# Two-layer attention and expert kernel on one Trainium2 core: the weighted sums of V of a step, in two halves of their columns behind the two pairs of scores

## The chip, the cores and the metric

The kernel runs on one core of one Trainium2 chip, as one program. The time is the device time of an execution in microseconds (us), taken on that core; three runs of the kernel before gave 772.68, 773.29 and 773.67 us, and the median of them, 773.29 us, is the time before. A profile of one execution stands beside them. Engines go by the short names of the profile: PE is TensorE's matmuls, PEld its weight loads, DVE is VectorE, ACT is ScalarE, POOL is GpSimd, SP is the engine that issues most of the DMAs.

## The reference

The input is one sequence of 1024 tokens with 256 features. Two layers run one after the other, each an attention block and a block of experts, with a layer norm ahead of and behind each block and a residual sum:

```
x = x + LN(attention0(LN(x)))      # 16 heads of 16, causal, with biases
x = x + LN(experts0(LN(x)))        # 32 experts, 4 per token, plus a shared one
x = x + LN(attention1(LN(x)))      # 16 heads of 16, causal, rotary positions
x = x + LN(experts1(LN(x)))        # RMS norm, 32 experts, 4 per token, shared one
```

The part that the change touches is the same in both attention blocks, for each head:

```
scores = q @ k.T / 4               # 1024 x 1024, only keys up to the query count
probs  = softmax(scores)
y      = probs @ v
```

## The kernel before, in words

Attention is cut into groups of four heads (`HG`) and chunks of 512 queries (`CH`). A phase is one group with one chunk, so there are four groups by two chunks = 8 phases (`PHASES`, numbered 0 to 7), and a step (`STEPS`) is one phase with one block of 128 keys. A phase of the first chunk has 4 steps, all on the diagonal, with 512, 384, 256 and 128 query columns; one of the second chunk has 8 steps, 4 of 512 columns and 4 on the diagonal, which stand by turns. That makes 48 steps in a layer.

For each step the scores stand transposed, keys by queries, in four banks of PSUM, one per head, made by `scores(st, p)` (L936 to L947) in two pairs of heads, p = 0 and 1. The first pair of a step waits until the exponentials of the first pair of the step before have emptied its two banks, the second pair likewise. ACT (`exps`, L1295 to L1302) turns each pair into probabilities with one instruction and writes them to one of three buffers `probs` (`PB`). On the diagonal POOL clears the upper triangle (L735). `weigh(st)` (L949 to L961) multiplies the probabilities by V: for each of the four heads the weights are V's block of 128 keys by 32 columns (16 of V, a column of ones, zeros), the moving operand is the probabilities of that head, and the result goes to 32 partitions of one bank (`RB`) that collects the sums of a whole phase. So the four heads of a step stand side by side in the array, 32 columns each. A matmul on 32-bit data is two instructions in the profile, so a `weigh` is 8 instructions of L959. After the last step of a phase ACT copies that bank to SBUF (`pv_copy`, L1304 to L1308), and the first `weigh` of the next phase waits for that copy.

Meanwhile the row maxima that the softmax needs are worked out a few phases ahead: a "max" unit (L865 to L881) is a product of queries and keys into one of three rotating banks, plus a small product that adds the causal mask (L880), and DVE reduces the bank to its maxima (L1563). Three banks means that PE can be at most three units ahead of DVE. Other units (`rows`, `turn`, `yT`, `proj`, `fT`, `logits`) go through the same three banks.

All this runs in an order written out once, by `schedule()` (L154 to L190). PE, ACT and DVE each walk through the same list and pick out their own part, and each engine works strictly in that order. For every step the list has: the scores of pair 0, one unit, the scores of pair 1, one unit, the `weigh` of the step two before (`HEAD_START` = 2), and then the remaining units of that step (3 to 5 in all while there are maxima left, `RATE`). ACT's copy at the end of a phase stands where the `weigh` of its last step stands in the list. In layer 0 the maxima run out at the end of phase 4; after that a step has at most one or two units.

```
        for p in range(2):
            if st < NSTEP:
                out.append(("score", st, p))
            out += more[:1]
            more = more[1:]
        if st >= HEAD_START:
            out.append(("weigh", st - HEAD_START))
        out += more
```

Of the kernel before, what the change touches and what calls it, by code (L numbers as in the profile page):

```python
# [21 lines left out]
HG = 4  # L22
NG = H // HG
CH = 512
# [129 lines left out]
def schedule():  # L154

    def maxima(g, c):
        return [("max", g, u) for u in range(CHUNK_UNITS[0] * c, CHUNK_UNITS[c])]

    own = maxima(0, 1) + [("rows", 0, 1)]
    out = maxima(0, 0) + [("rows", 0, 0)] + own[:OWN_AHEAD]
    own = own[OWN_AHEAD:]
    later = [x for g, c in PHASES[NC:] for x in maxima(g, c)]
    for st in range(NSTEP + HEAD_START):
        n, s = (STEPS[st][0], st - PHASE_AT[STEPS[st][0]]) if st < NSTEP else (NPH, st - NSTEP)
        more = []  # L170
        if n == 0 and s < TPC - 1:
            more, own = own[:FIRST_RATE], own[FIRST_RATE:]
        elif n == 0:
            more = own + later[:FIRST_MORE]
            later = later[FIRST_MORE:]
        elif n in RATE:
            more, later = later[:RATE[n]], later[RATE[n]:]
        more += [("rows", g, c) for (g, c), at in ROWS_AT.items() if at == (n, s)]
        if s == TURN_STEP and n >= 1:
            more.append(("turn", n - 1, 0))  # L180
        more += FRONT_AT.get((n, s), ())
        for p in range(2):
            if st < NSTEP:
                out.append(("score", st, p))
            out += more[:1]
            more = more[1:]
        if st >= HEAD_START:
            out.append(("weigh", st - HEAD_START))
        out += more
    return out  # L190

# [89 lines left out]
def build(nc, a, out):  # L281
    ctx = ExitStack()
    with ctx:
# [518 lines left out]
        def _(pe):  # L802
# [17 lines left out]
            for L in range(2):  # L820
# [125 lines left out]
                                       QA[0:KX, h, c * CH + off:(c + 1) * CH], start=True, stop=True)  # L946
                    mm.then_inc(S(f"sc{L}"), 1)  # L947

                def weigh(st):  # L949

                    n, g, c, b = STEPS[st]
                    off = max(0, b * P - c * CH)
                    pe.wait_ge(S(f"exp{L}"), 2 * st + 2)
                    if DIAGONAL[st]:
                        pe.wait_ge(S(f"masked{L}"), masked_steps(st))
                    if b == 0 and n >= 1:
                        pe.wait_ge(S(f"pv_sb{L}"), n)
                    for x in range(HG):
                        mm = pe.matmul(ps[32 * x:32 * x + 32, RB, off:CH], V[:, b, HG * g + x, :],  # L959
                                       probs[:, st % PB, x, off:CH], start=(b == 0), stop=(b == TPC * (c + 1) - 1))  # L960
                    mm.then_inc(S(f"pv{L}"), 1)  # L961

                for x in SCHEDULE:
                    if x[0] == "max" and x[2] == 0:
                        pe.wait_ge(S(f"qa_rows{L}_{x[1]}"), 16 * 2 * NPROD)
                    if x == ("score", 0, 0):
                        pe.wait_ge(S(f"v_sb{L}"), NT)
                        pe.wait_ge(S("v_pad"), 1 + 2 * L)
                        pe.wait_ge(S(f"qk_sb{L}"), 2 * KD * NC)
                        pe.wait_ge(S("k_ones"), 16 * NSH * (L + 1))  # L970
                    if x[0] == "score":
                        scores(*x[1:])
                    elif x[0] == "weigh":
                        weigh(x[1])
                    else:
                        unit(x)
                    if L == 0 and x[:2] == ("max", 0) and x[2] in LATE_K:
                        qk_product(*LATE_K[x[2]])
# [217 lines left out]
        def _(act):  # L1196
            for L in range(2):
# [112 lines left out]
                for x in SCHEDULE:  # L1310
                    if x[0] == "score":
                        exps(*x[1:])
                        if L == 1 and x[1:] == (0, 1):
                            split(1, 1, 0)
                        if x[1:] in ((1, 1), (2, 1)):
                            split(1, x[1] - 1, 1)
                    elif x[0] == "rows":
                        _, g, c = x
                        act.wait_ge(S(f"unit{L}"), UNIT_NO[x] + 1)
                        if g >= 1:  # L1320

                            act.wait_ge(S(f"max_rows{L}_{c}"), 16 * NSH * g)
                        nc.scalar.activation(mT[:, c * CH:(c + 1) * CH], ps[0:NSH * HG, UNIT_NO[x] % RB, :],
                                             ACT.Copy).then_inc(S(f"maxT{L}"), 1)
                        if g == 0:
                            act.wait_ge(S(f"maxT{L}"), c + 1)
                            max_rows(act, L, 0, c)
                        if (g, c) == (0, 0):
                            if L == 0:
                                qk_out(7)  # L1330
                                split(1, 1, 0)
                            else:
                                split(1, 0, 0)
                    elif x[0] == "weigh":
                        if x[1] + 1 in PHASE_AT:
                            pv_copy(STEPS[x[1]][0])
                srest, erest = SHARED[L] - SFULL[L] * P, HALF
                nsc = SFULL[L] + 1
# [748 lines left out]
```

## Time and profile before

| what | value |
|---|---|
| three runs, median | 773.29 us (772.68 to 773.67) |
| the profiled execution, span from first to last instruction | 771.2 us |
| median of the runs minus that span | 2.1 us |
| PE busy, share of the span | 674.1 us, 87% |
| PEld busy | 437.5 us, 57% |
| DVE busy | 485.2 us, 63% |
| ACT busy | 323.1 us, 42% |
| mean granted clock of TensorE | 0.954 |

No time of the profiled execution other than its span is shown; what lies around the span (start and end of the program) is taken as the 2.1 us by which the median of the runs is longer. The span falls into attention of layer 0 (to about 190 us), its experts (to about 415 us), attention of layer 1 (to about 600 us) and its experts. Busy matmuls are pipelined: a matmul's duration in the profile includes the time until its last result has come out, so two neighbours overlap, and the distance from one start to the next says how long the engine is really held.

### The profile page before, as it was taken

Reading aid. Unit: us, or ns where it says so; the run is one execution under the profiler, and the core shown is the slowest. Engines: PE = TensorE matmul, PEld = TensorE weight load, DVE = VectorE, ACT = ScalarE, POOL = GpSimd, SP = SyncE. Lnnn points to the kernel's source line nnn. Section 1 sums busy time; section 2 is a strip of 40 time slices with the busy share of each in tenths; the row PEclk is TensorE's granted clock in tenths of the full one; section 3 lists DMA queues with packets and bytes.
Section 4 is the critical chain, followed back from the end, with each engine's and each line's share of the span. In section 5 each row is a group of like instructions: output and inputs, shape, how many; then the busy total and the mean of one; then the engine's idle time right before and its main releaser. Section 6 shows DMA issues by size and latency. Waiting matters only on the chain.

```text
span 771.2 us, 13393 instructions
## 1 busy us (share of the span) xinstructions
PE 674.1 (87%) x4388; PEld 437.5 (57%) x4388; DVE 485.2 (63%) x1354; ACT 323.1 (42%) x684; POOL 249.5 (32%) x294
## 2 busy tenths in 40 slices
PE   3988999999569999999983978999998899999991
PEld 2533443344437899999962533343343455999980
DVE  4389899544683344444476788899527886243457
ACT  3553464765124233222241533565676231333322
POOL 3041011210137677444430083011211002767630
PEclk9999999999778999999995979999999999999995
DMA  3433210060008999999780245003000540399762
GB/s 99 135 124 126 77 34 2 5 216 28 27 1 262 303 328 327 294 311 315 261 267 0 75 144 165 15 2 115 2 2 1 164 133 14 116 291 308 244 204 91
DMA packets 60294, 108.60 MB, mean 141 GB/s; under 512 B 11194, under 2 KB 37131, under 8 KB 60100
## 3 DMA queue, kind: packets, MB, share of 16 engines
q1 hardware_dynamic: 52532, 93.86, 37.4%
q0 software_dynamic: 7632, 13.86, 5.5%
q8 instruction: 37, 0.61, 0.3%
q14 instruction: 29, 0.24, 0.1%
q10 hardware_dynamic: 64, 0.03, 0.0%
HBM read 79.98 MB, written 19.79 MB: 129 GB/s over the span
## 4 chain that ended last, share of the span: by engine, by line
PE 61%; DVE 26%; ACT 4%; DMA 4%; issue 3%; SPq 1%; ACTq 0%; DVEq 0%; POOLq 0%
PE ps L1132 17%; DVE mx L1563 11%; PE ps L959 7%; PE ps L945 5%; PE ps L1145 5%; PE ps L1147 5%; PE ps L877 5%; PE ps L991 4%; PE ps L1071 3%; ACT X L1301 2%; PE ps L1103 2%; DVE X L1960 2%; PE ps L832 1%; PE ps L910 1%; SPq L545 1%
## 5 line engine op out<-in xcount | busy, mean ns | idle before, releaser
L1563 DVE TENSOR_REDUCE mx<-ps 128x1 f32<-128x512 f32 (+3 forms) x304 | 180.2, 656 | 24.7 <-PE ps L880 17.4
L1301 ACT ACTIVATE X<-ps 128x1024 f32<-128x1024 f32 (+1 forms) x192 | 146.5, 809 | 87.1 <-PE ps L945 86.6
L763 POOL DMA_INDIRECT outs<-X,token x95 | 95.2, 1002 | 77.2 <-DVE X L1940 63.4
L877 PE MATMUL ps<-KA,QA 112*128 112x512 bf16 (+3 forms) x384 | 110.8, 338 | 9.8 <-DVE mx L1563 4.4
L735 POOL TENSOR_SCALAR_AFFINE_SELECT X<-X 128x512 f32<-128x512 f32 x64 | 40.8, 638 | 218.1 <-ACT X L1301 218.1
L1132 PE MATMUL ps<-QA,KA 128*128 x756 | 96.0, 277 | 2.5 <-issue 2.1
L945 PE MATMUL ps<-QA,KA 114*128 114x512 bf16 (+3 forms) x384 | 93.0, 327 | 5.6 <-ACT X L1301 3.9
L1132 PEld LDWEIGHTS ps<-QA,KA 128*128 128x128 f32 x756 | 92.9, 193 | 5.1 <-issue 3.4
L1927 DVE TENSOR_TENSOR X<-ps,X 128x128 f32<-128x128 f32 x95 | 27.7, 292 | 105.3 <-ACT X L1418 103.9
L755 POOL DMA_INDIRECT V<-token_rows,row_of_slot x64 | 65.8, 1028 | 68.4 <-DVE row_of_slot L1841 42.9
L877 PEld LDWEIGHTS ps<-KA,QA 112*128 112x128 bf16 x384 | 36.2, 98 | 85.6 <-DVE mx L1563 61.8
L959 PE MATMUL ps<-X,V 128*32 128x512 f32 (+3 forms) x768 | 81.1, 497 | 0.6 <-ACT X L1308 0.4
L1416 ACT ACTIVATE X<-ps 128x128 f32<-128x128 f32 x95 | 26.4, 278 | 118.8 <-PE ps L1132 117.8
L1145 PE MATMUL ps<-KA,X 128*128 128x256 f32 x190 | 57.6, 385 | 1.1 <-DVE X L1940 0.8
L945 PEld LDWEIGHTS ps<-QA,KA 114*128 114x128 bf16 x384 | 30.1, 98 | 49.2 <-ACT X L1301 30.8
L1147 PE MATMUL ps<-X 128*128 128x256 f32 x190 | 56.7, 380 | 0.0
L991 PE MATMUL ps<-xT,w_sgu 128*128 128x512 f32 x112 | 53.0, 617 | 2.2 <-DVE QA L1708 2.2
L1940 DVE COPY X<-ps 128x256 f32<-128x256 f32 x95 | 40.4, 425 | 20.8 <-DMA outs<-X,token 18.0
L880 PE MATMUL ps<-mask_q,identb 128*128 128x128 bf16 x256 | 50.0, 225 | 0.0
L1132 PE MATMUL ps<-X,KA 128*128 128x128 f32 x384 | 48.2, 275 | 0.3 <-ACT X L1407 0.3
L1132 PEld LDWEIGHTS ps<-X,KA 128*128 128x128 f32 x384 | 45.6, 192 | 0.6 <-ACT X L1407 0.5
L1147 PEld LDWEIGHTS ps<-X 128*128 128x128 f32 x190 | 36.4, 192 | 5.0
(298 smaller groups left out, 868.9 us busy)
## 6 DMA issues: line engine op xcount, KB each, us to landing
KA<-in_ex SPq DMA_DIRECT2D x95, 512.0 KB, 4.1
X<-in_dn SPq DMA_DIRECT2D x95, 64.0 KB, 4.9
outs<-empty SPq DMA_DIRECT2D x4, 1024.0 KB, 10.1
V<-outs SPq DMA_DIRECT2D x4, 1024.0 KB, 6.3
QA<-X SPq DMA_DIRECT2D x28, 128.0 KB, 2.5
KA<-X SPq DMA_DIRECT2D x28, 128.0 KB, 2.5
QA<-w_sdn SPq DMA_DIRECT2D x28, 128.0 KB, 2.5
KA<-parts_k SPq DMA_DIRECT2D x28, 128.0 KB, 2.5
```

The source lines that it names most:

```text
L755: pool.indirect_dma_start(out=rows[:, g % ROW_RING, :], out_offset=None, in_=token_rows[L], in_offset=bass.IndirectOffsetOnAxis(ap=row_of_ ...
L763: pool.indirect_dma_start(out=outs[L], out_offset=bass.IndirectOffsetOnAxis(ap=token[L][:, i:i + 1], axis=0), in_=erows[:, g % OUT_RING, : ...
L877: mm = pe.matmul(ps[:, bank, j * w:(j + 1) * w], QA[0:KQ, h, i * P:(i + 1) * P], KA[0:KQ, h, s0:s0 + w], start=True, stop=not diag)
L880: mm = pe.matmul(ps[:, bank, (j + 1) * w - P:(j + 1) * w], identb[:, :], mask_q[:, :], start=False, stop=True)
L945: mm = pe.matmul(ps[:, 4 + 2 * p + x, off:CH], KA[0:KX, h, b * P:(b + 1) * P], QA[0:KX, h, c * CH + off:(c + 1) * CH], start=True, stop=True)
L959: mm = pe.matmul(ps[32 * x:32 * x + 32, RB, off:CH], V[:, b, HG * g + x, :], probs[:, st % PB, x, off:CH], start=(b == 0), stop=(b == TPC ...
L991: mm = pe.matmul(ps[:, up_bank(L, u, x), :], w_sgu[:, k, col:col + P], xT[:, k, n * CH:(n + 1) * CH], start=(k == 0), stop=(k == KD - 1))
L1132: mm = pe.matmul(ps[:, 2 + g % RING, m * P:(m + 1) * P], w_ex[:, r, col:col + P], rowsT_all[:, k, bass.ds(at, P)] if L == 0 else rowsT(L, ...
L1145: pe.matmul(ps[:, 6 + g % 2, 0:D], eact[:, g % RING, 0:P], w_ex[:, r, KD * UPC * P:EW], start=True, stop=False)
L1147: mm = pe.matmul(ps[:, 6 + g % 2, 0:D], eact[:, g % RING, P:2 * P], w_rest[:, r // 2, :], start=False, stop=True)
L1301: nc.scalar.activation(probs[:, st % PB, 2 * p:2 * p + 2, off:CH], ps[:, 4 + 2 * p:6 + 2 * p, off:CH], ACT.Exp, scale=SCALE).then_inc(S(f" ...
L1563: v.tensor_reduce(mx[:, part, i, h0:h0 + nh], ps[:, n % RB, 0:nh * w].rearrange("p (h w) -> p h w", h=nh), AX.X, ALU.max)\
```

## The change

The `weigh` of a step becomes two, with half of the query columns each: `mid` is the middle between the first column that counts and 512, half 0 goes from the first column to `mid`, half 1 from `mid` to 512. In the list half 0 stands behind pair 0 of the scores (and the unit behind it), half 1 behind pair 1. Each half is four matmuls on the same weights as before. The waits (both exponentials of the step, the mask, and at the first step of a phase ACT's copy) all stand at half 0; the semaphore that tells that a step is done is raised by half 1. ACT's copy at the end of a phase stays behind pair 1.

```
-        if st >= HEAD_START:
-            out.append(("weigh", st - HEAD_START))
+            if st >= HEAD_START:
+                out.append(("weigh", st - HEAD_START, p))
         out += more
...
-                def weigh(st):
+                def weigh(st, half):
 
                     n, g, c, b = STEPS[st]
                     off = max(0, b * P - c * CH)
-                    pe.wait_ge(S(f"exp{L}"), 2 * st + 2)
-                    if DIAGONAL[st]:
-                        pe.wait_ge(S(f"masked{L}"), masked_steps(st))
-                    if b == 0 and n >= 1:
-                        pe.wait_ge(S(f"pv_sb{L}"), n)
+                    if half == 0:
+                        pe.wait_ge(S(f"exp{L}"), 2 * st + 2)
+                        if DIAGONAL[st]:
+                            pe.wait_ge(S(f"masked{L}"), masked_steps(st))
+                        if b == 0 and n >= 1:
+                            pe.wait_ge(S(f"pv_sb{L}"), n)
+                    mid = (off + CH) // 2
+                    t0, t1 = ((off, mid), (mid, CH))[half]
                     for x in range(HG):
-                        mm = pe.matmul(ps[32 * x:32 * x + 32, RB, off:CH], V[:, b, HG * g + x, :],
-                                       probs[:, st % PB, x, off:CH], start=(b == 0), stop=(b == TPC * (c + 1) - 1))
-                    mm.then_inc(S(f"pv{L}"), 1)
+                        mm = pe.matmul(ps[32 * x:32 * x + 32, RB, t0:t1], V[:, b, HG * g + x, :],
+                                       probs[:, st % PB, x, t0:t1], start=(b == 0 and half == 0),
+                                       stop=(b == TPC * (c + 1) - 1 and half == 1))
+                    if half == 1:
+                        mm.then_inc(S(f"pv{L}"), 1)
...
                     elif x[0] == "weigh":
-                        if x[1] + 1 in PHASE_AT:
+                        if x[1] + 1 in PHASE_AT and x[2] == 1:
                             pv_copy(STEPS[x[1]][0])
```

## Rows read from the trace of the kernel before

**Rows 1.** the page: span; busy us, share, instructions by engine

```profile
span 771.2 us, 13393 instructions
...
PE 674.1 (87%) x4388; PEld 437.5 (57%) x4388; DVE 485.2 (63%) x1354; ACT 323.1 (42%) x684; POOL 249.5 (32%) x294
```

**Rows 2.** chain of waits, 54 to 190 us, shares by line

```profile
by line: DVE mx L1563 23.9%; PE ps L959 21.7%; PE ps L945 16.7%; PE ps L877 11.9%; ACT X L1301 6.3%; PE ps L892 2.6%; PE ps L910 2.5%; PE ps L880 2.5%; issue 2.4%; PE ps L898 1.4%; PE ps L991 1.4%; PE ps L886 1.4%; PE ps L931 1.3%; DVE nb L
```

**Rows 3.** busy us by stretch, layer 0, phases 1 to 7

```profile
core 0: us, PE busy (x) PEld busy (x) DVE busy (x) ACT busy (x) POOL busy (x), PEclk, DMA share, GB/s
67.48:94.96 27.48, 25.80 (x201) 10.90 (x199) 25.11 (x48) 14.46 (x19) 2.55 (x4) 1.00 0.27 83
94.96:104.24 9.28, 9.28 (x81) 4.39 (x79) 8.33 (x18) 5.69 (x9) 2.55 (x4) 1.00 0.01 2
104.24:131.15 26.91, 25.64 (x184) 10.15 (x182) 25.16 (x47) 14.58 (x19) 3.01 (x5) 1.00 0.08 25
131.15:140.65 9.50, 9.50 (x78) 3.97 (x76) 8.32 (x15) 6.04 (x10) 2.55 (x4) 1.00 0.01 2
140.65:147.82 7.17, 6.22 (x55) 2.07 (x52) 2.32 (x9) 5.58 (x9) 2.14 (x4) 1.00 0.00 1
147.82:167.41 19.59, 18.73 (x134) 8.39 (x131) 6.68 (x14) 13.78 (x18) 2.33 (x5) 1.00 0.66 215
167.41:186.16 18.75, 18.01 (x145) 7.05 (x141) 11.23 (x49) 13.35 (x17) 3.17 (x5) 1.00 0.09 29
```

**Rows 4.** groups of instructions on the page: busy, mean ns | idle before

```profile
L959 PE MATMUL ps<-X,V 128*32 128x512 f32 (+3 forms) x768 | 81.1, 497 | 0.6 <-ACT X L1308 0.4
```

**Rows 5.** PE in time: start us, us, line, tile; two weighs

```profile
96.33 0.27 PE L877 MATMUL ps<-KA,QA 112*128 112x256 bf16 x1
96.45 0.22 PE L880 MATMUL ps<-mask_q,identb 128*128 128x128 bf16 x1
96.60 1.06 PE L959 MATMUL ps<-X,V 128*32 128x512 f32 x8
97.59 0.34 PE L877 MATMUL ps<-KA,QA 112*128 112x384 bf16 x1
...
98.87 0.22 PE L880 MATMUL ps<-mask_q,identb 128*128 128x128 bf16 x1
99.02 0.43 PE L959 MATMUL ps<-X,V 128*32 128x128 f32 x8
99.38 0.34 PE L877 MATMUL ps<-KA,QA 112*128 112x384 bf16 x1
```

**Rows 6.** PE in order of time: the last three weighs of layer 0

```profile
184.46 1.77 PE L959 MATMUL ps<-X,V 128*32 128x256 f32 x24
186.16 1.13 PE L991 MATMUL ps<-xT,w_sgu 128*128 128x512 f32 x2
```

**Rows 7.** PE in order of time: the turn from phase 6 to 7

```profile
171.10 0.60 PE L945 MATMUL ps<-QA,KA 114*128 114x512 bf16 x2
172.01 0.61 PE L945 MATMUL ps<-QA,KA 114*128 114x512 bf16 x2 [0.31 <-ACT X L1301]
172.59 1.07 PE L959 MATMUL ps<-X,V 128*32 128x512 f32 x8
173.59 0.50 PE L945 MATMUL ps<-QA,KA 114*128 114x384 bf16 x2
```

**Rows 8.** ACT in order of time: exponentials, and the copy ending phase 6

```profile
153.05 3.35 ACT L1301 ACTIVATE X<-ps 128x1024 f32<-128x1024 f32 x4
...
171.84 0.60 ACT L1308 ACTIVATE X<-ps 128x512 f32<-128x512 f32 x1
```

**Rows 9.** PE in order of time: layer 1, phase 7, ahead of fT

```profile
588.55 0.60 PE L945 MATMUL ps<-QA,KA 114*128 114x512 bf16 x2
590.90 0.63 PE L923 MATMUL ps<-identf,xn 128*128 128x128 f32 x4 [1.75 <-DVE xn L1637]
```

**Rows 10.** DVE in order of time: a reduction that waited behind a weigh

```profile
120.72 1.89 DVE L1563 TENSOR_REDUCE mx<-ps 128x1 f32<-128x512 f32 x3 [0.47 <-PE ps L880]
```

## What the change will do to the time: the prediction

> **What bounds the kernel now.** I read the page first. PE is busy for 674.1 of 771.2 us [rows 1], but that is an average over four blocks, and the change touches attention alone, so the second view is the chain of waits from 54 to 190 us, attention of layer 0. The reader is to see that no engine owns it: the reductions of DVE hold 23.9% of the chain, the weighs (L959) 21.7%, the scores (L945) 16.7% [rows 2]. The third view cuts this by phases [rows 3], and says who binds where. In phases 2 and 4 PE is busy from end to end (9.28 of 9.28, 9.50 of 9.50 us). In phases 1 and 3 PE and DVE are both near full: PE 25.80 and 25.64, DVE 25.11 and 25.16, of 27.48 and 26.91 us. From phase 5 on DVE has little to do, and PE is busy for 6.22 of 7.17, 18.73 of 19.59 and 18.01 of 18.75 us. What is left there are waits for ACT, which in places runs exponentials back to back (four in 3.35 us [rows 8]). The granted clock is 1.00 in all seven, so TensorE ran at 2.4 GHz, and the change takes no work from PE that could slow it. So PE has almost nothing spare: any time that PE is held longer counts, unless it falls into one of these few waits.
>
> **What a weigh costs beyond its columns.** The fourth view is PE in order of time around two weighs [rows 5]. A weigh of 512 columns holds PE from 96.60 to 97.59, 0.99 us, one of 128 columns from 99.02 to 99.38, 0.36. That is (0.99 - 0.36) / 3 = 0.21 us for each 128 columns and 0.15 that doesn't depend on them. Ahead of it there is a second loss: L880 starts at 96.45 and the weigh at 96.60, 0.15 us later, though its 128 columns need only 0.06 (L877 ahead of it takes 0.12 for 256). So 0.09 us going in and 0.15 coming out, 0.24 us for each turn from full-width matmuls to the four 32-column ones and back. It is the turn that costs, not the eight instructions: the last three weighs of the layer (256, 512 and 128 columns, 24 instructions) stand one behind the other and hold PE from 184.46 to 186.16, 1.70 us [rows 6]; their columns are 7 x 0.21 = 1.47 and one turn out 0.15, so the two joints cost 0.04 each.
>
> The Trainium skill, "TensorEngine Tiling (Array Packing)", Tiling Modes, says that changing the tiling mode drains TensorE, and "TensorE: Matmul & The Clock Gate", Single matmul latency, puts a warm matmul's time beyond its columns at 398 cycles, an estimate of 0.17 us a drain and 0.33 for both directions. By the page a turn would cost 0.33 us, by the rows it costs 0.24; the rows decide, and the page's price is the second rival below.
>
> **The change part by part.** It removes no column: the same columns go through PE in two parts, at 0.21 per 128. It adds four matmuls (eight instructions) to each of 96 weighs (768 instructions of L959, eight each [rows 4]), and a second turn wherever the second pair of scores stands between the halves. That is 46 of 48 steps in each layer; the last two steps have no scores left beside them, so their halves cost a joint of 0.04. 92 x 0.24 = 22.1 us more of PE over both layers. Halves of 64 columns occur, and no row shows a weigh of that width: it lies between 0.15 (no columns) and 0.36 (128), and I take 0.15 + 0.11 = 0.26 by the line.
>
> What hides it is what PE waits today. A stretch of rows 3 holds as many weighs as its phase has steps: 8, 4, 8, 4, 4, 8, 8. Layer 0, added turns against idle PE:
> - phase 0: two turns, on a chain of DVE and DMA: 0;
> - phase 1: 8 x 0.24 = 1.9 against 27.48 - 25.80 = 1.68 idle: 0.2;
> - phase 2: 1.0 against 0: 1.0;
> - phase 3: 1.9 against 26.91 - 25.64 = 1.27: 0.6;
> - phase 4: 1.0 against 0: 1.0;
> - phase 5: 1.0 against 0.95, of which I let two thirds be of use: 0.3;
> - phase 6: 1.9 against 0.86: 1.1;
> - phase 7: 1.9 against 0.74: 1.2.
>
> That is 5.4 us. It counts every idle moment of PE as cover, which errs low, and gives nothing for the tails that the busy time includes, which errs high.
>
> The change also moves a wait. The first weigh of a phase waits for ACT's copy of the bank, and this wait now stands ahead of the second pair of scores. Between phases 6 and 7 the first pair starts at 171.10, the second waits until 172.01 for its banks, and the weigh starts at 172.59 [rows 7]; ACT's copy runs from 171.84 to 172.44 [rows 8]. With the change half 0 can start at 172.44 + 0.09 = 172.53 and holds PE for 0.15 + 2 x 0.21 = 0.57. The second pair, no longer at 172.01, starts at 173.10 and holds PE for 0.49 (172.01 to 172.59, less 0.09 of going in), so half 1 starts at 173.68 and comes out at 174.25. Before, that point came at 173.59: 0.66 later, of which 0.24 is the turn already counted, so 0.42 for the moved wait. Behind it on PE stand the second pair, a unit and half 1, and ACT waits for that pair. There are seven such places in a layer. In the phases with maxima, PE has units to do until the copy is made, and the wait costs between 0 and this 0.42. I take 0.4 at two of the seven and 0.6 for the other five together: 1.4 us a layer. The bounds are 0 and 7 x 0.42 = 2.9. The waits for the exponentials cost nothing by moving: the first pair of a step already waits for a later exponential than half 0 does. The mask of POOL is made behind that earlier exponential too. No DMA is moved, SP's and POOL's queues keep their order, and ACT's copy keeps its place in ACT's list.
>
> What the change gives back: the largest piece of PE work between two units shrinks from a whole weigh to a half, so DVE starves less (it stood 0.47 us before the reduction at 120.72, behind a weigh [rows 10]), and a half fills the wait of the second pair for its banks. Both are in the sum only as cover, since in these phases PE then is the later one: with DVE fed earlier, PE itself is late next.
>
> Layer 0 comes to 5.4 + 1.4 = 6.8 us. In layer 1 the same, except in phase 7: there PE waits 1.75 us for the norm ahead of fT at 590.90 [rows 9], behind six of the eight weighs, so six turns and the moved wait go into that wait. Phase 7 costs 2 x 0.24 = 0.5 in place of 1.2 + 0.4: layer 1 comes to 5.7. Behind attention everything hangs on its last product, expert weights too, so the delay passes on whole. The sum is 12.5; I round it down to 12 for the DVE waits that shrink. On the profiled execution's own time (771.2 us of span and 2.1 around it, which is the median of the runs, 773.3) that is **785.3 us**, 1.6% slower; call it 785.
>
> **The rivals.**
> 1. Nothing is covered: the waits of PE reappear at other places, as in-order engines with three banks between them do not trade idle time freely. For it: in phases 1 and 3 both engines are over 90% busy, and two such engines rarely interlock better. Against: PE's waits for ACT stand exactly where half 0 goes. Price 22.1 + 2.8 for the moved waits = 24.9: 798 us.
> 2. A turn costs both tails in full. L880 is 0.22 us long while its columns need 0.06, a tail of 0.16, so 0.32 a turn if nothing of it overlaps. The half is shorter than anything in rows 5, which speaks for it; the line through 128 and 512 columns speaks against. 92 x 0.08 = 7.4 more, four fifths of it uncovered: 785 + 6 = 791 us. The pages of the Trainium skill named above give nearly the same price, 0.33.
> 3. Faster: DVE is the true bound in phases 1 to 4, and a weigh in one piece starves it. Its idle time there is 2.37 + 0.95 + 1.75 + 1.18 = 6.25 us a layer. If halves feed it evenly, half of that comes back: 773.3 - 6.2 = 767 us. It decides if 24 more turns fit into PE's idle 1.68 + 1.27 = 2.95 us of these phases, that is if a turn costs below 0.12 us. Rows 5 say 0.24, and phases 2 and 4 show no idle PE at all.
> 4. No change: the covers and the smoother feeding balance the turns to within 1.5 us. 773 us.
>
> **How the numbers follow.** The forecast has 0.62 (its own range 777 to 790), rival 1 has 0.08, rival 2 has 0.10, rival 3 has 0.12, rival 4 has 0.08. What a measurement of this kernel can tell from no change is 0.2%, 1.5 us. Slower by more: 0.62 + 0.08 + 0.10 = 0.80; faster by more 0.12; within it 0.08. The range for 8 in 10 runs from 773, which leaves out rival 3 and part of rival 4, to 796, which leaves out rival 1.
>
> **What would show it.** L959 has 1536 instructions. Around a half of 256 columns PE is held 0.57 us, with about 0.09 ahead of it, and so twice in each step. Each of phases 2 and 4 grows from 9.28 and 9.50 us by 1.0 us or a little more, while phase 1 stays at about 27.5. In phase 7 of layer 1 the wait for fT shrinks from 1.75 us to nearly nothing. At the start of a phase PE waits for L1308 in more than two places. The experts' blocks keep their lengths. It would be wrong if a half of 256 columns held PE for less than 0.45 us or lost nothing going in, or if phases 1 and 3 got shorter by more than 1 us each because DVE no longer waits.

## The result, and the profile after

The changed kernel takes 792.82 us (median of 4 runs, 790.43 to 793.59), the kernel before 773.48 beside it (4 runs, 772.68 to 775.13): a ratio of 1.0233, 95% interval 1.0198 to 1.0269. It is slower, as forecast, but by 19 us where 12 had been forecast: inside the range of 773 to 796, outside the forecast's own 777 to 790.

The page of the profiled execution (793.21 us, span 791.5), answering [rows 1, 4]; the third line here is the chain of waits by engine over the whole span:

```profile
span 791.5 us, 14929 instructions
...
PE 695.5 (88%) x5156; PEld 450.7 (57%) x5156; DVE 488.7 (62%) x1354; ACT 330.0 (42%) x684; POOL 249.7 (32%) x294
...
PE 69%; DVE 20%; ACT 3%; DMA 3%; issue 3%; SPq 1%; ACTq 0%; DVEq 0%; POOLq 0%
...
L962 PE MATMUL ps<-X,V 128*32 128x256 f32 (+3 forms) x1536 | 101.1, 337 | 7.1 <-ACT X L1313 7.0
```

The weighs (L962 now) are 1536 instructions and 20.0 us dearer (101.1 against 81.1), and ACT's copy of the bank (L1313 now) keeps PE waiting 7.0 us ahead of them where it was 0.4. In the chain through attention of layer 0, answering [rows 2], the weighs and scores have grown, and DVE's reductions have gone from 23.9% to 8.9%:

```profile
by line: PE ps L962 28.0%; PE ps L945 22.3%; PE ps L877 16.9%; DVE mx L1568 8.9%; PE ps L880 3.9%; ACT X L1306 3.1%; PE ps L892 2.7%; issue 2.5%; PE ps L910 2.4%; ACT X L1313 2.0%; PE ps L886 1.9%; PE ps L898 1.3%; PE ps L931 1.3%; PE ps L9
```

Phases 1 to 7 of layer 0, answering [rows 3] line by line (span of the stretch, then busy time of each engine):

```profile
68.63:96.86 28.23, 27.40 (x265) 11.85 (x264) 25.38 (x47) 15.25 (x19) 2.54 (x4) 1.00 0.24 75
96.86:107.38 10.52, 10.34 (x113) 4.89 (x111) 8.73 (x18) 6.02 (x9) 2.54 (x4) 1.00 0.01 2
107.38:135.81 28.43, 27.14 (x248) 10.94 (x246) 25.76 (x47) 15.30 (x19) 2.94 (x5) 1.00 0.08 24
135.81:146.59 10.78, 10.53 (x110) 4.44 (x108) 8.54 (x15) 6.48 (x10) 2.60 (x5) 1.00 0.00 1
146.59:154.47 7.88, 6.89 (x86) 2.56 (x84) 2.56 (x9) 5.66 (x9) 1.90 (x3) 1.00 0.01 2
154.47:175.98 21.51, 20.20 (x199) 9.20 (x195) 6.55 (x15) 14.06 (x19) 3.03 (x4) 1.00 0.60 197
175.98:197.03 21.05, 19.84 (x225) 8.50 (x221) 10.96 (x48) 14.09 (x18) 3.17 (x5) 1.00 0.08 26
```

Every phase is longer, by 0.75, 1.24, 1.52, 1.28, 0.71, 1.92 and 2.30 us: 9.72 in all. PE's busy time grew by 9.16 us (113.18 to 122.34 over the seven rows) and its idle time from 5.50 to 6.06. So PE is held longer, and none of that went into its idle time on balance. The granted clock is 1.00 in all seven, as before, so none of it is the clock. Layer 1, cut the same way and at 1.00 as well, grew by 8.5 us. Phase 0 is 1.1 and 1.2 us longer in the two layers, and the two stretches behind phase 7 (the experts, and what leads up to the next phase 0 or to the end) are together 0.2 us shorter (268.4 and 176.3 against 270.9 and 174.0), which makes up the 20.3 us between the two spans.

PE in order of time around half weighs, answering [rows 5]:

```profile
72.53 0.22 PE L880 MATMUL ps<-mask_q,identb 128*128 128x128 bf16 x1
72.68 0.32 PE L962 MATMUL ps<-X,V 128*32 128x64 f32 x8
72.93 0.61 PE L945 MATMUL ps<-QA,KA 114*128 114x512 bf16 x2
...
90.66 0.22 PE L880 MATMUL ps<-mask_q,identb 128*128 128x128 bf16 x1
90.81 0.64 PE L962 MATMUL ps<-X,V 128*32 128x256 f32 x8
91.38 0.60 PE L945 MATMUL ps<-QA,KA 114*128 114x512 bf16 x2
```

A half of 256 columns holds PE for 0.57 us (90.81 to 91.38), one of 64 for 0.25, with 0.15 from L880 to the weigh ahead of both: the predicted 0.57, 0.26 and 0.15.

PE at the turn from phase 6 to 7, answering [rows 7], with two other places where half 0 waits for the copy, and the wait for fT in layer 1, answering [rows 9]:

```profile
151.20 0.64 PE L962 MATMUL ps<-X,V 128*32 128x256 f32 x8 [0.89 <-ACT X L1313]
...
159.94 0.64 PE L962 MATMUL ps<-X,V 128*32 128x256 f32 x8 [1.31 <-ACT X L1313]
...
179.91 0.61 PE L945 MATMUL ps<-QA,KA 114*128 114x512 bf16 x2
181.40 0.64 PE L962 MATMUL ps<-X,V 128*32 128x256 f32 x8 [0.89 <-ACT X L1313]
181.97 0.60 PE L945 MATMUL ps<-QA,KA 114*128 114x512 bf16 x2
182.51 0.64 PE L962 MATMUL ps<-X,V 128*32 128x256 f32 x8
183.08 0.50 PE L945 MATMUL ps<-QA,KA 114*128 114x384 bf16 x2
...
607.86 0.63 PE L923 MATMUL ps<-identf,xn 128*128 128x128 f32 x4 [0.21 <-DVE xn L1642]
```

ACT in order of time at that turn, answering [rows 8]; the wait in the last line is new:

```profile
178.83 1.94 ACT L1306 ACTIVATE X<-ps 128x1024 f32<-128x1024 f32 x2
180.66 0.60 ACT L1313 ACTIVATE X<-ps 128x512 f32<-128x512 f32 x1
181.13 1.04 ACT L1306 ACTIVATE X<-ps 128x1024 f32<-128x1024 f32 x1
182.62 1.81 ACT L1306 ACTIVATE X<-ps 128x1024 f32<-128x1024 f32 x2 [0.44 <-PE ps L945]
```

From the first pair to the point behind half 1 it takes 183.08 - 179.91 = 3.17 us; from the first pair to the point behind the weigh it took 2.49 [rows 7]. That is 0.68 more; the prediction worked out 0.66. The copy keeps half 0, half 0 keeps the second pair, and ACT then stands 0.44 us for that pair.

DVE's longer waits in phases 1 and 3, in order of time, answering [rows 10] (four of the fifteen):

```profile
81.12 0.56 DVE L1568 TENSOR_REDUCE mx<-ps 128x1 f32<-128x384 f32 x1 [0.53 <-PE ps L880]
82.02 1.49 DVE L1568 TENSOR_REDUCE mx<-ps 128x1 f32<-128x384 f32 x3 [0.34 <-PE ps L880]
85.30 0.69 DVE L1568 TENSOR_REDUCE mx<-ps 128x1 f32<-128x512 f32 x1 [0.57 <-PE ps L877]
86.19 3.83 DVE L1568 TENSOR_REDUCE mx<-ps 128x1 f32<-128x512 f32 x6 [0.20 <-PE ps L877]
```

The wait behind one whole weigh has become two, one behind half 0 and a pair of scores, one behind half 1. Such waits of 0.15 us and more in the two phases were 7 with 3.18 us before and are 15 with 4.61 us.

### The profile page after: what moved, and what is told of

It reads as the page before. It is cut to its first block, busy times and chain, and to the rows that moved or that the text cites. A ratio compares the mean times of both kernels' runs of the same rounds, so it can differ in the third digit from the quotient of the medians.

```text
span 791.5 us, 14929 instructions
## 1 busy us (share of the span) xinstructions
PE 695.5 (88%) x5156; PEld 450.7 (57%) x5156; DVE 488.7 (62%) x1354; ACT 330.0 (42%) x684; POOL 249.7 (32%) x294
## 4 chain that ended last, share of the span: by engine, by line
PE 69%; DVE 20%; ACT 3%; DMA 3%; issue 3%; SPq 1%; ACTq 0%; DVEq 0%; POOLq 0%
PE ps L1137 16%; PE ps L962 10%; PE ps L945 8%; PE ps L877 7%; DVE mx L1568 6%; PE ps L1150 5%; PE ps L1152 5%; PE ps L996 4%; PE ps L1076 3%; PE ps L832 2%; PE ps L1108 2%; DVE X L1965 2%; PE ps L880 1%; PE ps L910 1%; PE ps L931 1%
## 5 line engine op out<-in xcount | busy, mean ns | idle before, releaser
L1568 DVE TENSOR_REDUCE mx<-ps 128x1 f32<-128x512 f32 (+3 forms) x304 | 183.7, 656 | 32.7 <-PE ps L880 21.9
L1306 ACT ACTIVATE X<-ps 128x1024 f32<-128x1024 f32 (+1 forms) x192 | 153.3, 810 | 104.2 <-PE ps L945 102.6
L877 PE MATMUL ps<-KA,QA 112*128 112x512 bf16 (+3 forms) x384 | 113.5, 348 | 6.7 <-DMA KA<-X 2.8
L962 PE MATMUL ps<-X,V 128*32 128x256 f32 (+3 forms) x1536 | 101.1, 337 | 7.1 <-ACT X L1313 7.0
L945 PE MATMUL ps<-QA,KA 114*128 114x512 bf16 (+3 forms) x384 | 96.2, 332 | 1.2 <-DMA QA<-mT 0.9
L962 PEld LDWEIGHTS ps<-X,V 128*32 128x32 f32 x1536 | 30.9, 108 | 60.5 <-issue 46.6
L996 PE MATMUL ps<-xT,w_sgu 128*128 128x512 f32 x112 | 54.6, 633 | 2.2 <-DVE QA L1713 2.2
L1945 DVE COPY X<-ps 128x256 f32<-128x256 f32 x95 | 40.3, 424 | 23.9 <-DMA outs<-X,token 21.5
L880 PE MATMUL ps<-mask_q,identb 128*128 128x128 bf16 x256 | 53.0, 234 | 0.0
L945 PEld LDWEIGHTS ps<-QA,KA 114*128 114x128 bf16 x384 | 25.2, 98 | 47.7 <-issue 31.2
```

Source lines behind the costliest of these rows:

```text
L877: mm = pe.matmul(ps[:, bank, j * w:(j + 1) * w], QA[0:KQ, h, i * P:(i + 1) * P], KA[0:KQ, h, s0:s0 + w], start=True, stop=not diag)
L880: mm = pe.matmul(ps[:, bank, (j + 1) * w - P:(j + 1) * w], identb[:, :], mask_q[:, :], start=False, stop=True)
L945: mm = pe.matmul(ps[:, 4 + 2 * p + x, off:CH], KA[0:KX, h, b * P:(b + 1) * P], QA[0:KX, h, c * CH + off:(c + 1) * CH], start=True, stop=True)
L962: mm = pe.matmul(ps[32 * x:32 * x + 32, RB, t0:t1], V[:, b, HG * g + x, :], probs[:, st % PB, x, t0:t1], start=(b == 0 and half == 0), sto ...
L996: mm = pe.matmul(ps[:, up_bank(L, u, x), :], w_sgu[:, k, col:col + P], xT[:, k, n * CH:(n + 1) * CH], start=(k == 0), stop=(k == KD - 1))
L1306: nc.scalar.activation(probs[:, st % PB, 2 * p:2 * p + 2, off:CH], ps[:, 4 + 2 * p:6 + 2 * p, off:CH], ACT.Exp, scale=SCALE).then_inc(S(f" ...
```

## The experiments

The expectations set the theory of turns (the prediction's: 92 added turns, partly covered) against rivals that each text spells out. Ratios are to the kernel before on the same chip, with 95% intervals. In all of them the columns computed stay the same; only the order or the cutting of the weighs changes. The diffs with two halves rest on the changed kernel's `weigh`; those with a whole weigh rest on the kernel before; in two of these a mark `weighed` says where ACT's copy is due. A line of dots stands for parts of a diff that are left out.

**Both halves where the whole weigh was**, one behind the other: the change's instructions without its added turns.

```
-            if st >= HEAD_START:
-                out.append(("weigh", st - HEAD_START, p))
+        if st >= HEAD_START:
+            out += [("weigh", st - HEAD_START, half) for half in range(2)]
```

> Both halves of each weigh stand behind the second pair, one behind the other: the 768 added instructions stay, no turn from wide to 32-column matmuls is added, no wait moves. Theory of the turns (each passage of PE into the 32-column matmuls and out again costs 0.24 us): only 96 joints of 0.04 us are added, 3.8 us, so 775 to 778 us against 773.5 of before. Rival A, the added instructions themselves cost: 788 to 795 us, as slow as the change. Rival B, the moved wait and the later second pair of scores cost: 773 to 775 us.

774.44 us, ratio 0.9997 [0.9970, 1.0024]. The 768 added instructions and their joints cost nothing that can be measured, so the 19 us come from where the halves stand. The theory of turns had 775 to 778 us, with 0.04 for each joint; two joined halves of 256 columns hold PE from 465.49 to 466.49 us in this trace, 1.00 us where the whole weigh took 0.99 [rows 5], so that price was too high.

**The whole weigh ahead of the second pair**, ACT's copy staying behind it: the change's place without cutting.

```
-        if st >= HEAD_START:
-            out.append(("weigh", st - HEAD_START))
+            if st >= HEAD_START:
+                out.append((("weigh", "weighed")[p], st - HEAD_START))
...
```

> The weigh stays whole, but stands behind the first pair of scores; ACT's copy keeps its place. No added turn and no added instruction, but the wait for ACT's copy stands ahead of the second pair, and the second pair comes later. Theory of the turns: only the moved wait counts, of which the changed kernel's trace shows 3.5 us a layer in place of 0.2, partly instead of other waits: 775 to 781 us. Rival A (instructions): 773 us but for the wait. Rival B (order and moved wait are the whole cost): 786 to 793 us.

797.5 us, 1.0290 [1.0242, 1.0337]: not better than the change, with not one turn added. The theory of turns missed this. The place ahead of the second pair has a price of its own. Not all of the 23 us need be that: the granted clock was 0.92 in phases 6 and 7 of layer 0 of this profiled execution, where it was 1.00 before and with the change.

**The change, but the first step of each phase keeps both halves behind the second pair**: no moved wait.

```
             if st >= HEAD_START:
-                out.append(("weigh", st - HEAD_START, p))
+                if st - HEAD_START not in PHASE_AT:
+                    out.append(("weigh", st - HEAD_START, p))
+                elif p == 1:
+                    out += [("weigh", st - HEAD_START, half) for half in range(2)]
```

> The change, but at the first step of every phase both halves stand joined behind the second pair, so the wait for ACT's copy is back in its old place and 14 of the 92 added turns go. Theory of the turns: 14 x 0.24 = 3.4 us less, and of the 6.6 us that PE waits longer for the copy in both layers up to all: 783 to 789 us against 792.8 of the change. If the moved wait costs nothing: 789 to 790 us. Rival A (instructions): 792 to 793 us.

786.12 us, 1.0145 [1.0098, 1.0193], as expected and 6.7 below the change. Phases 5 to 7 of layer 0:

```profile
143.93:151.34 7.41, 6.81 (x86) 2.72 (x83) 2.56 (x9) 5.55 (x9) 1.90 (x3) 1.00 0.00 0
151.34:172.17 20.83, 20.09 (x199) 9.36 (x195) 6.54 (x15) 13.82 (x19) 3.02 (x4) 1.00 0.62 203
172.17:192.55 20.38, 19.74 (x225) 8.67 (x221) 10.97 (x48) 13.90 (x18) 3.24 (x5) 1.00 0.08 27
```

PE's idle time in these phases falls from 3.51 to 1.98 us and that in phases 2 and 4 from 0.43 to 0: 1.96 us a layer for the moved wait, beside seven turns. Where PE still waits in the late phases, in order of time:

```profile
156.24 0.61 PE L948 MATMUL ps<-QA,KA 114*128 114x512 bf16 x2 [0.74 <-ACT X L1309]
...
177.02 0.60 PE L948 MATMUL ps<-QA,KA 114*128 114x512 bf16 x2 [0.31 <-ACT X L1309]
```

These are the waits for exponentials of the kernel before, at the same two places and as long (0.74 in a row below, 0.31 in [rows 7]), with seven added turns in each of the two phases.

**The change from phase 5 on only**, joined halves ahead of that.

```
-                out.append(("weigh", st - HEAD_START, p))
+                if st >= PHASE_AT[5]:
+                    out.append(("weigh", st - HEAD_START, p))
+                elif p == 1:
+                    out += [("weigh", st - HEAD_START, half) for half in range(2)]
```

> The halves stand apart only from phase 5 on, where the maxima have run out; before that they are joined behind the second pair. Theory of the turns: the changed kernel's phases 5 to 7 are 4.9 and 3.4 us longer than before, and the joints of the earlier phases add 56 x 0.04 = 2.2 us: 781 to 785 us. As my prediction had it (2.6 + 0.9 and 1.9 us in these phases): 778 to 781 us. If DVE hides the turns of phases 1 to 4, nearly the whole loss lies in the late phases: 789 to 793 us.

781.56 us, 1.0087 [1.0058, 1.0117], as expected: the late phases make about 7 of the 19 us, phases 0 to 4 the rest.

**Fewer turns**: two whole weighs together behind every second step, everywhere and (with `PHASE_AT[5]` in place of 0) from phase 5 on only.

```
-    for st in range(NSTEP + HEAD_START):
+    for st in range(NSTEP + HEAD_START - 1):
...
-        if st >= HEAD_START:
-            out.append(("weigh", st - HEAD_START))
+        if HEAD_START <= st < 0:
+            out.append(("weigh", st - HEAD_START))
+        elif st >= HEAD_START and st % 2 == 0:
+            out += [("weigh", st - HEAD_START + x) for x in range(2)]
```

> The reverse of the change: the weighs of two steps stand whole, one behind the other, behind every second step. 24 turns of 48 go in each layer. Theory of the turns: 48 x 0.24 = 11.5 us less on PE, the joints cost 48 x 0.04 = 1.9 us, but a lump of up to 2 us lets DVE run dry in the phases with maxima: 764 to 772 us. If turns cost nothing: 774 to 785 us.

> Weighs by twos only from phase 5 on, where no maxima are left. 20 turns go in all. Theory of the turns: 20 x 0.2 = 4 us less, part of which ACT's waits take: 769 to 773 us against 774. If turns cost nothing: 774 to 778 us.

786.93 us, 1.0201 [1.0141, 1.0262], and 779.67 us, 1.0075 [1.0038, 1.0112]. Both expected a gain and missed. In the first, phases 1 and 3 of layer 0 have four turns less each, but PE's busy time there does not fall (26.08 and 25.79 us after 25.80 and 25.64), and its idle time rises from 1.68 and 1.27 to 2.44 and 2.68 us. In the second, the idle time in phases 6 and 7 rises from 0.86 and 0.74 to 2.12 and 2.08. Lumps of weighs keep DVE or ACT without work, and PE then waits for them: DVE stands 1.22 and 1.27 us at a time in phase 1 of the first (at most 0.72 before), ACT 2.76 us in phase 6 of the second. This last wait is part clock: ahead of it two weighs hold PE for 3.35 us, while the granted clock goes down to 0.50 (1.2 GHz). So the two runs show what lumps cost, not what a turn is worth.

**Two halves behind the second pair with one unit between them**: the added turns without the change's place.

```
         if st >= HEAD_START:
-            out.append(("weigh", st - HEAD_START))
+            out += [("weigh", st - HEAD_START, 0)] + more[:1] + [("weigh", st - HEAD_START, 1)]
+            more = more[1:]
```

> Half 0 stands where the whole weigh stood, half 1 one unit later where that step has a unit left (26 steps of a layer, all in phases 0 to 4), joined otherwise. Nothing of the weigh stands ahead of the second pair, no wait moves, only 52 turns are added. Theory of the turns: 52 x 0.24 = 12.5 us on PE, of which DVE hides some: 779 to 785 us against 774 of before. Theory that the loss comes from work and waits put ahead of the second pair: 772 to 775 us.

775.92 us, 1.0036 [1.0020, 1.0053]; the theory of turns expected 779 or more and missed, and so did, by less, its rival's 772 to 775. Phases 1 to 4 of layer 0 (phases 1, 3, 2, 4):

```profile
66.67:93.94 27.27, 27.02 (x264) 12.06 (x263) 25.60 (x49) 14.47 (x19) 2.55 (x4) 1.00 0.25 80
104.25:130.71 26.46, 26.41 (x248) 11.56 (x246) 25.21 (x47) 14.55 (x19) 3.01 (x5) 1.00 0.09 26
93.94:104.25 10.31, 10.31 (x113) 4.89 (x111) 8.66 (x18) 5.79 (x9) 2.55 (x4) 1.00 0.01 2
130.71:140.99 10.28, 10.28 (x109) 4.65 (x108) 8.83 (x16) 6.14 (x10) 2.55 (x4) 1.00 0.00 1
```

Where PE is full, four added turns cost 1.03 and 0.78 us, so 0.26 and 0.20 each: the price was right. In phases 1 and 3 sixteen turns vanish into 0.25 and 0.05 us of remaining idle time, and the phases are a little shorter than before. So the cover was there; the change did not reach it.

**The whole weigh ahead of the second pair but for the first step of a phase**: its place without the moved wait.

```
-        if st >= HEAD_START:
-            out.append(("weigh", st - HEAD_START))
+            if st >= HEAD_START:
+                late = st - HEAD_START in PHASE_AT
+                if p == late:
+                    out.append(("weigh", st - HEAD_START))
+                if p == 1:
+                    out.append(("weighed", st - HEAD_START))
...
```

> The weigh whole and behind the first pair, but at the first step of a phase behind the second pair as before, so the wait for ACT's copy has not moved and no turn is added. If the 23 us of the whole early weigh came from the moved wait (8.5 us shown at the copy, with what follows from it): 776 to 782 us. If from the place of the lump, between the two pairs, after which four units in a row meet three banks: 785 to 792 us.

783.95 us, 1.0146 [1.0102, 1.0190]. With no added turn and no moved wait this still loses 11 us. Phases 1 and 3 of layer 0, with PE idle for 2.35 and 2.14 us:

```profile
66.86:95.54 28.68, 26.33 (x201) 10.88 (x200) 25.36 (x49) 15.14 (x19) 2.55 (x4) 1.00 0.25 76
...
104.95:133.24 28.29, 26.15 (x185) 9.97 (x183) 25.15 (x47) 15.21 (x19) 3.16 (x6) 1.00 0.08 24
```

The weigh ahead of the second pair leaves four units in a row behind that pair. PE runs into the three full banks there (it waits for DVE ahead of the fourth unit, 0.20 us at 80.54 and 0.35 at 84.85), and DVE stands while PE does weigh and scores (0.96 and 1.00 us at a time, where it was 0.72 and 0.62 before). This gave theory C: the spacing of the units decides how much idle time can be used. It does not account for all of the loss: of 5.5 us in phases 1 to 7 of layer 0, phases 1 and 3 make 2.6 and phase 7, which has no maxima, 2.2; PE waits there 0.87 us for DVE at 186.70 and 0.27 for POOL at 190.70.

**The change with half 1 one unit later**: the same turns, the same moved wait, another spacing.

```
             if st >= HEAD_START:
+                if p == 1:
+                    out += more[:1]
+                    more = more[1:]
                 out.append(("weigh", st - HEAD_START, p))
```

> As the change, but half 1 stands one unit of the head-ready list further back, so that at most three units follow one another behind the second pair of scores; half 0 stays ahead of the second pair. The number of turns stays as in the change. Theory C (the idle time of PE did not serve as cover in the change because half 0 ahead of the second pair leaves the units in one row, in which PE still meets three full banks): PE's idle time in phase 1 of layer 0 (0.83 us in the change) stays or falls, phases 1 and 3 become shorter by 0.3 to 0.8 us each, phases 2 and 4 by 0.2 or less, and the whole comes to 787 to 791 us. Rival D (the cover was lost to the place of half 0 alone, the row of units behind the second pair has no part in it): 792 to 793.5 us, as the change.

785.84 us, 1.0160 [1.0128, 1.0192]: 7 us below the change, somewhat more than theory C had given, and rival D falls. Phases 1 and 3 of layer 0:

```profile
66.63:93.95 27.32, 27.02 (x265) 12.20 (x264) 25.43 (x49) 15.23 (x19) 2.54 (x4) 1.00 0.28 88
104.54:131.31 26.77, 26.59 (x248) 11.24 (x246) 24.65 (x46) 15.29 (x19) 2.94 (x5) 1.00 0.09 26
```

PE is idle for 0.30 and 0.18 us in place of 0.83 and 1.29. Over both layers phases 1 and 3 give back 5.5 us (in layer 1 they are 27.31 and 26.77). Phase 0 of layer 0 is 1.3 us shorter too, at a granted clock of 1.00; the last section has why that part is not the order's.

**Halves with a unit between them in phases 1 and 3 alone.**

```
         if st >= HEAD_START:
-            out.append(("weigh", st - HEAD_START))
+            between = more[:1] if n in (1, 3) else []
+            out += [("weigh", st - HEAD_START, 0)] + between + [("weigh", st - HEAD_START, 1)]
+            more = more[len(between):]
```

> Two halves with one unit between them, both behind the second half-step as the whole weigh was, in phases 1 and 3 alone; elsewhere the halves stand together. 32 added turns in both layers, 32 x 0.24 = 7.7 us of PE if nothing hid them. Theory C (a turn is hidden where it falls into time that PE is idle anyway, and even spacing keeps DVE fed): phases 1 and 3 are no longer than before, by the run with turns behind pair 1 shorter by 0.2 and 0.45 us each, so 772 to 774 us. Rival A (turns cost their 0.24 us each wherever they stand, less the 1.7 and 1.3 us of idle time that one phase has): 775 to 777 us.

773.88 us, 1.0000 [0.9977, 1.0022], as theory C expected: 32 added turns without a price that can be measured.

**The whole weigh one unit later, and two units later, in phases 1 and 3**: no halves, no added turn. The diff is for one unit; for two it has `more[:2]` and `more[2:]`.

```
+        if n in (1, 3):
+            out += more[:1]
+            more = more[1:]
         if st >= HEAD_START:
             out.append(("weigh", st - HEAD_START))
```

> As the kernel before, but in phases 1 and 3 the whole weigh stands one unit later, with no added turn and no halves: what the place of the weigh among the units is worth by itself. Theory C (the spacing of the units decides how much of PE's and DVE's idle time is used): PE's idle time of 1.68 and 1.27 us in phases 1 and 3 of layer 0 changes by at least 0.4 us, and the time moves with it, 770 to 773 us if a more even spacing helps, at most 775. Rival (the place among the units is worth nothing): 773 to 774 us with the phases of before within 0.1 us.

> As the kernel before, but in phases 1 and 3 the whole weigh stands two units later (one unit later gave 0.9934 of before: phases 1 and 3 of layer 0 became 26.27 and 25.72 us, from 27.48 and 26.91). In PE's time a score pair needs about 0.49 us, a whole weigh with its turn 1.1, a unit 0.37, so the gaps from unit to unit in a step are 0.86, 0.86, 1.5, 0.37, 0.37 before, 0.86, 0.86, 0.37, 1.5, 0.37 with the weigh one unit later, and 0.86, 0.86, 0.37, 0.37, 1.5 with it two units later; from an even supply (0.79 each) they stray by at most 0.85, 0.71 and 0.84. Theory C (the spacing of the units sets how much of PE's and DVE's idle time is used): most of the gain is lost again, phases 1 and 3 are within 0.5 us of before, 772 to 775 us, ratio 0.998 to 1.001. Rival (the gain came from the weigh meeting its exponentials or its banks later, whatever the spacing): as with one unit or shorter, phases 1 and 3 at most 26.3 and 25.8 us, 766 to 770 us.

One unit later: 769.03 us (6 runs), 0.9934 [0.9912, 0.9956], faster than both kernels, by 5 us against the one before and a little below what theory C had given. Two units later: 773.88 us, 1.0002 [0.9981, 1.0024], the gain gone, as theory C had it and its rival had not. Phases 1 and 3 of layer 0 with one unit:

```profile
66.12:92.39 26.27, 25.50 (x200) 10.90 (x199) 25.02 (x49) 14.35 (x19) 2.54 (x4) 1.00 0.24 78
101.67:127.40 25.73, 25.18 (x185) 10.27 (x182) 25.07 (x47) 14.54 (x19) 3.00 (x5) 1.00 0.10 26
```

and with two:

```profile
67.46:94.71 27.25, 26.08 (x200) 11.19 (x199) 25.55 (x49) 14.46 (x19) 2.54 (x4) 1.00 0.26 81
104.00:130.40 26.40, 25.31 (x185) 10.32 (x183) 25.71 (x48) 14.64 (x19) 3.00 (x5) 1.00 0.08 25
```

With one unit both engines are idle less than before: PE 0.77 and 0.55 us, DVE 1.25 and 0.66. With two PE is idle for 1.17 and 1.09, and the two phases are still 0.23 and 0.51 us shorter than before; over both layers that is 1.5 us, inside what the interval leaves open.

## Why the prediction was right in sign and wrong in size

**Right: the price of a turn.** Half weighs hold PE as worked out, phases without idle time pay 0.20 to 0.26 us a turn, and over phases 1 to 7 the 44 added turns cost 9.16 / 44 = 0.21 us of PE's busy time. The Trainium skill, "TensorEngine Tiling (Array Packing)", Tiling Modes, has TensorE drain when the tiling mode changes; the turn in the rows agrees with that. The estimate of 0.33 us that the prediction worked out from the Trainium skill, "TensorE: Matmul & The Clock Gate", Single matmul latency, does not agree with the 0.20 to 0.26, and the measurement decides. Rival 2 falls as a cause with the measured price, though 791 us is nearer to the result than 785.

**Wrong: the cover.** The step that failed is "It counts every idle moment of PE as cover, which errs low". For layer 0 the prediction had 10.6 us of turns, 5.2 of them covered, and 1.4 for the moved wait: 6.8. Measured are 9.2 of turns and 2.0 for the moved wait (the run without it), so with 9.7 in all only 1.4 was covered. That the turns had been put 1.4 us too high hid as much of the miss, by luck. In layer 1 the same working gives 9.3 of turns, 8.5 in all and 2.7 covered, where 5.7 had been forecast. Most of that cover is the one wait that was used as predicted: the wait for fT fell by 1.54 us, and phase 7 of layer 1 grew by 0.78 where 0.5 had been forecast. Phase 0, at which the prediction put nothing, adds 2.3 us over both layers, with the clock lower there (last section). Two things were overlooked about the cover, and both can be read in the kernel before. Its longer waits of PE in phase 3 and in the late phases, in order of time:

```profile
107.68 0.39 PE L886 MATMUL ps<-identb,nb 128*8 128x128 bf16 x4 [0.21 <-DVE mx L1563]
117.29 0.66 PE L892 MATMUL ps<-identf,X 128*128 128x128 f32 x4 [0.35 <-DVE mx L1563]
121.46 0.39 PE L886 MATMUL ps<-identb,nb 128*8 128x128 bf16 x4 [0.23 <-DVE mx L1563]
...
152.72 0.60 PE L945 MATMUL ps<-QA,KA 114*128 114x512 bf16 x2 [0.74 <-ACT X L1301]
...
178.42 0.39 PE L945 MATMUL ps<-QA,KA 114*128 114x256 bf16 x2 [0.28 <-ACT X L1301]
```

In the late phases the idle time is not spread over the steps. In phase 6 it is one wait, 0.74 of 0.86 us, 5 us into the phase; what is added behind it on PE has nothing to hide in. Nor does a turn ahead of a wait help where it also delays the scores that ACT needs: in the run without the moved wait this one is still 0.74, and 1.98 of the 2.55 us of phases 5 to 7 stay unused. And the wait of 0.31 at 172.01 [rows 7] was counted twice: as cover in phase 7, and again in the moved wait, whose working already lets the second pair come later than 172.01.

In phases 1 and 3 PE waits for DVE, and that end moves when DVE is fed later. The change's waits in phase 3:

```profile
111.12 0.39 PE L886 MATMUL ps<-identb,nb 128*8 128x128 bf16 x4 [0.35 <-DVE mx L1568]
...
121.46 0.65 PE L892 MATMUL ps<-identf,X 128*128 128x128 f32 x4 [0.35 <-DVE mx L1568]
...
125.88 0.39 PE L886 MATMUL ps<-identb,nb 128*8 128x128 bf16 x4 [0.23 <-DVE mx L1568]
```

The same units wait, as long as before or longer, though eight turns were added to the phase: PE's idle time there is 1.29 us after 1.27. In phase 1 half of it was used, 0.83 is left of 1.68. The prediction said that DVE would starve less behind halves; it starves more (3.18 us in those waits before, 4.61 after), since half 0 delays the second pair and the unit behind it, and half 1 the next. That it is the order and not the halves is shown: moving half 1 by one unit leaves 0.18 us of idle time in phase 3, and halves behind the second pair leave 0.05.

**The moved wait** was worked out rightly where it was worked out (0.68 against 0.66 from the first pair on), but "0.6 for the other five together" was too little. PE waits for the copy at five places in each layer, 0.18, 0.25, 0.89, 1.31 and 0.89 us in layer 0, and three of them are in the late phases, where ACT has exponentials back to back ahead of its copy.

**The rivals.** Rival 1, nothing covered, is nearest as a mechanism: its sentence that PE's waits "reappear at other places" is what phase 3 shows, though 1.4 and 2.7 us of the two layers were covered. Rival 3, DVE as the bound that an even supply relieves, is false of the change but was half a truth about the kernel: the whole weigh one unit later takes 0.7% from the time by this means, without halves. Rival 4, no change, falls: the interval begins at 1.0198.

**The signs that were named.** 1536 instructions, 0.57 us around a half, the copy's wait at more than two places (10) and the wait for fT down from 1.75 to 0.21 us came as written; phases 2 and 4 grew by 1.24 and 1.28, 0.18 and 0.25 of it the copy's wait. The stretches with the experts did not keep their lengths one by one (2.5 us shorter and 2.3 longer), only in sum. Phase 1 was to stay at about 27.5 us and became 28.23: this sign pointed at the cover.

**What stays open.** That added turns ahead of a late wait delay ACT's exponentials by as much is argued from the unchanged 0.74, not shown apart. The rule of spacing was formed on the first eight runs; four later orders tested it, and their effect was read in phases 1 and 3 alone. What the early weigh costs in phase 7 it does not explain.

## What to carry to other kernels

Idle time of an engine covers added work only if that work stands ahead of the wait in the engine's own order and doesn't delay whoever ends the wait: look up each wait and its place, and don't sum a phase's idle time. Where two engines feed one another through a few buffers, write the order as a list of gaps between the handovers and even these out; here moving one unit past an unchanged weigh was worth 5 us, and moving two was worth nothing. Use a wait once: either as cover, or in the working of a step that is moved.

## What the hardware showed that was not expected

PE waits 2.06 us for DVE near 60 us in both profiled executions. In the one of before the granted clock stays at 1.00 (2.4 GHz) behind it; in the changed kernel's it is 0.50 (1.2 GHz) from 62 to 68 us, in which single matmuls of L880 take 0.31 us in place of 0.22, and phase 0 is 1.1 us longer. The runs with half 1 one unit later and with the first step joined kept 1.00 in that stretch, and the run with halves in phases 1 and 3 alone, which takes as long as the kernel before, had 0.60 there. The plainest case is the run with the whole weigh one unit later: up to 66 us its list is that of the kernel before, it waits 2.06 us as well, and it had 0.63 and 0.52 from 62 to 64 and 64 to 66 us. So this belongs to the execution and not to the change. In phase 0 of layer 1, 1.2 us longer at 0.86 against 0.99, it is alike: the runs with joined halves and with the change from phase 5 on only have the same list there, and behind a wait of 2.06 us one kept 1.00 and the other went down to 0.50. The 2.3 us are part of the 20.3 between the two profiled spans, and of their spread from run to run.
